# VectorE's eviction of the own-rows product moved behind the copy of the next turned tile, in a graph network with three layers on one core

## The reference

```python
deg = jnp.maximum(segment_sum(ones, dst), 1.0)
h = layernorm(x)
for l in range(3):
    h_neigh = segment_sum(h[src], dst) / deg
    rst = relu(h @ W_self[l] + h_neigh @ W_neigh[l] + b[l])
    h = rst / max(norm(rst), 1e-12)
x = x + h
# then per row: layer norm, gate over 8 experts, the best two of them, layer norm
```

## Time and profile before

| | before |
|---|---|
| median of 3 runs | 2106.8 us (2105.93 to 2120.68) |
| profiled execution, time | 2109.54 us |
| profiled execution, span | 2107.5 us |
| granted TensorE clock, mean | 0.990 |
| TensorE matmul busy | 1983.7 us, 94% |
| VectorE busy | 1673.1 us, 79% |
| ScalarE busy | 1019.9 us, 48% |
| GpSimd busy | 1274.4 us, 60% |

### The profile page before, as it was taken

How to read it: one execution, slowest core, us unless ns; L and a number is a source line. 1 busy time by engine, 2 the same in 40 slices (tenths; PEclk the granted TensorE clock), 3 DMA queues, 4 the chain that set the end, 5 groups by cost and what they waited for, 6 DMA issues and landing times.

```text
span 2107.5 us, 43053 instructions
## 1 busy us (share of the span) xinstructions
PE 1983.7 (94%) x14767; PEld 1098.9 (52%) x14773; DVE 1673.1 (79%) x4118; ACT 1019.9 (48%) x1801; POOL 1274.4 (60%) x1396
## 2 busy tenths in 40 slices
PE   6999899997999999999999999998899999999996
PEld 2444444443444444444444444444577777777774
DVE  7678986655777777776888878885699999999985
ACT  4444333333344344443444444554677776777751
POOL 2884116774566666664444444444578888888865
PEclk9999999998999999999999999999999999999999
DMA  6664348984887877864878887765778999899963
GB/s 205 171 169 132 123 139 135 145 126 113 194 195 195 189 202 194 193 191 148 244 245 250 245 250 234 223 219 184 216 165 176 176 186 170 178 179 180 172 100 49
DMA packets 307454, 379.27 MB, mean 180 GB/s; under 512 B 176825, under 2 KB 176999, under 8 KB 307239
## 3 DMA queue, kind: packets, MB, share of 16 engines
q1 hardware_dynamic: 246423, 211.09, 42.2%
q0 software_dynamic: 60816, 165.43, 32.1%
HBM read 175.81 MB, written 165.31 MB: 162 GB/s over the span
## 4 chain that ended last, share of the span: by engine, by line
PE 45%; POOL 24%; issue 12%; DVE 8%; DMA 7%; ACT 4%; SPq 0%; POOLq 0%; DVEq 0%; ACTq 0%
PE psY L580 20%; PE psS L580 18%; DMA w_n<-HH 5%; POOL out_dram L924 4%; POOL node_info L759 4%; POOL X L852 3%; PE psT L1799 2%; POOL zr L915 2%; POOL slot_table L759 2%; POOL G L836 2%; POOL area L836 2%; PE psY L1900 1%; POOL scl L905 1%; DVE R L1495 1%; PE psA L1859 1%
## 5 line engine op out<-in xcount | busy, mean ns | idle before, releaser
L580 PE MATMUL psY<-w_n,HT 128*128 128x512 f16 x1884 | 438.8, 383 | 31.6 <-DVE HT L1369 22.0
L580 PE MATMUL psS<-w_s,HT 128*128 128x512 f16 x1884 | 432.2, 379 | 0.0
L580 PEld LDWEIGHTS psY<-w_n,HT 128*128 128x128 f16 x1884 | 183.1, 99 | 265.2 <-DVE HT L1369 33.2
L1015 ACT ACTIVATE RR<-R 128x512 f32<-128x512 f32 x237 | 149.5, 631 | 311.3 <-DVE R L1495 311.2
L580 PEld LDWEIGHTS psS<-w_s,HT 128*128 128x128 f16 x1884 | 180.3, 98 | 199.4 <-issue 0.5
L868 POOL DMA_INDIRECT y_rows<-YB,poutT x158 | 161.8, 1024 | 197.8 <-DVE YB L1376 162.9
L1386 DVE SCALAR_TENSOR_TENSOR SB<-psS,downs,bias 128x512 f32<-128x512 f32 x237 | 177.7, 750 | 65.6 <-PE psS L580 64.8
L580 PE MATMUL psS<-w_w,raw 128*128 128x512 f16 x948 | 217.5, 379 | 0.8 <-ACT raw L1108 0.8
L861 POOL TENSOR_TENSOR scl<-ssm,halfpow 128x1 f32<-128x1 f32 x158 | 88.9, 562 | 195.0 <-DVE ssm L1513 195.0
L1376 DVE SCALAR_TENSOR_TENSOR YB<-psY,YB 128x512 f16<-128x512 f32 x237 | 162.6, 686 | 50.3 <-ACT YB L982 50.3
L1026 ACT ACTIVATE HH<-RR,scl 128x512 f16<-128x512 f32 x158 | 114.0, 722 | 150.4 <-POOL scl L861 150.4
(11 more groups left out here) (312 smaller groups left out, 4085.0 us busy)
## 6 DMA issues: line engine op xcount, KB each, us to landing
self_rows<-SB SPq DMA_DIRECT2D x236, 256.0 KB, 2.7
Sl<-self_rows SPq DMA_DIRECT2D x158, 256.0 KB
area<-in_x_dram SPq DMA_DIRECT2D x78, 256.0 KB, 4.1
y_rows<-YB SPq DMA_DIRECT2D x78, 256.0 KB
out_dram<-obb SPq DMA_DIRECT2D x78, 256.0 KB, 4.2
raw<-in_L_gnn_W_neigh_dram SPq DMA_DIRECT2D x12, 256.0 KB, 3.4
raw<-in_L_gnn_W_self_dram SPq DMA_DIRECT2D x12, 256.0 KB, 3.8
y_rows<-YB,poutT POOLq DMA_INDIRECT x158
```

The source lines that it names most:

```text
L580: mm = eng.matmul(acc, lhs[:, a, c, :], w[:, bpart, c, :], start=(c == 0 and n == 0), stop=(stop and c == KC - 1 and n == 2))
L1015: act.activation(RR[i][:, :], R[i][:, :], ACT.Relu).then_inc(s.rr, 1)
```

## The change

In the plans of VectorE for layers 1 and 2, `sev_early` is taken from the end of the list, where it had tile s, to the place behind `turn`, with tile s-1. In each step VectorE so evicts the own rows of the tile before, after it has made the one-hot matrix and copied the turned rows of tile s+1. The plan gets one step more at its end. Nothing else is changed.

```diff
-                run_plan(T, [(5, lambda t, l=l: one_hot(t, l)), (1, lambda t, l=l: turn(t, l)),
+                run_plan(T, [(5, lambda t, l=l: one_hot(t, l)), (1, lambda t, l=l: turn(t, l)), (-1, lambda t, l=l: sev_early(t, l)),
                                       (2, lambda t, l=l: hlo(t, l)), (0, lambda t, l=l: ylo(t, l)), (3, lambda t, l=l: carry_lo(t, l)),
                                       (3, lambda t, l=l: combine(t, l)), (3, lambda t, l=l: sum_squares(t, l)),
-                                      (3, lambda t, l=l: sum_floor(t, l)), (0, lambda t, l=l: sev_early(t, l))],
+                                      (3, lambda t, l=l: sum_floor(t, l))],
                          late_steps, run=l - 1)
```

## The result

| | before | changed |
|---|---|---|
| median of 11 runs | 2106.05 us (2102.48 to 2120.68) | 2125.65 us (2119.16 to 2131.31) |
| profiled execution, time | 2109.54 us | 2120.55 us |
| profiled execution, span | 2107.5 us | 2118.5 us |

The ratio of the two is 1.0081, with a 95% interval of 1.0067 to 1.0094: 0.8% slower, some 17 us. The profiled execution is one of the faster ones of the changed kernel; in it the loss is 11.0 us, so what follows places 11 of the 17 us.

What follows compares the result with a forecast made beforehand. TensorE was taken to bound the early parts, a loop without TensorE nearly to close the late ones. Terms -2.3 + 6 + 3 + 3 = +9.7 us on 2106.8 gave 2116.5, say 2117 us; range 2101 to 2131.

Steps and rivals of the forecast that it cites:

- Late parts: -2.3 forecast: Late parts: 1.0 us gained over 20 pairs, 1.3 us at the two layer ends; ends -13.2 and 0.
- A loop without TensorE: Late parts: a chain over power, hhi, late turn, yhi, ylo, carry, combine, only 0.05 us a pair shorter than TensorE's loop.
- rival (b): Late parts: the copy is the bound after all, gaining 13.2 us; about 2106 us; chance 0.08.
- Early layer 1: +6 and +3 forecast: Early layer 1: +6 us for DMA transposes issued later, +3 us for the store nearer ahead on their queue.
- the feedback: Early layer 1: a late transpose gives the next 7.02 us lead, afterwards 6.34; losing this costs +6 us, ends 0 and +9.2.
- Rival (a): Early parts: transposes behind a wait land under 6.34 us, in layer 2 under 5.7, so no loss; 2104.5 us; chance 0.17.
- The term that I had cut to a tenth: Early layer 1: the store 0.84 us nearer ahead of the transpose on SyncE's queue, +3 us, ends 0 and +28.6.
- Early layer 2: +3 forecast: Early layer 2: SyncE issues the transpose 0.61 us later, behind store, load and bias write; +3 us, ends 0 and 14.6.
- the fixed landing: Early layer 2: only the issue moves; no loss if transposes land 5.7 us after issue or sooner.
- Rival (c): Early layer 2: transposes have no slack, each pair takes 0.6 us more; 2128 us; chance 0.13.
- The upper end of 28.6 us: Early layer 1: all 34 odd tiles' transposes let the nearer store pass, at 0.84 us each.

Runs made afterwards that it cites:

- experiment 4: The kernel before with sev behind turn in the late parts alone, early parts as before: ratio 0.9985 (0.9968 to 1.0001).
- experiment 8: The kernel before with only ScalarE's yhi moved ahead of the late turn: ratio 1.0005 (0.9995 to 1.0015).
- experiment 1: The kernel before with sev behind turn in layer 1 alone, layer 2 as before: ratio 1.0043 (1.0026 to 1.0060).
- experiment 3: The changed kernel with SyncE's store of own rows behind the DMA transpose in both layers: ratio to the kernel before 0.9994 (0.9978 to 1.0009).
- experiment 9: The kernel before with the store of even tiles in layer 1 held back to stand near the transpose: ratio 1.0055 (1.0036 to 1.0074).
- experiment 2: The kernel before with sev behind turn in layer 2 alone, layer 1 as before: ratio 1.0037 (1.0021 to 1.0052).
- experiment 5: The kernel before with only SyncE's store of own rows moved behind the DMA transpose, both layers: ratio 1.0033 (1.0020 to 1.0045).
- experiment 7: The kernel before with sev behind turn in the late parts alone and ScalarE's yhi ahead of the late turn: ratio 0.9982 (0.9972 to 0.9992).
- experiment 10: The changed kernel with GpSimd's gather behind the scatter in layer 1's first 64 steps: ratio to the kernel before 0.9997 (0.9987 to 1.0006).

## Why the prediction came out as it did

The forecast was +9.7 us, 2117 us, 0.5% slower. The runs show 0.8%, some 17 us, 2125.65 us in the median; the one profile shows +11.0. The direction held, and the rows foretold which instruction would stand where. That the terms add up to nearly what the profile shows is in part luck: layer 1 was put 2.3 us too high and layer 2 3.3 us too low, and neither size came from the mechanism as I had given it.

**Late parts: -2.3 forecast, -2.1 measured.** A loop without TensorE closes them; pairs fell by 0.06 us, not 0.66. The critical view shows the change from one loop to the other, experiments 4 and 8 agree, and rival (b) is out. The wait for the copy fell to 0.65 us only, where I expected about 0.4.

**Early layer 1: +6 and +3 forecast, +6.7 measured (+8.0 in experiment 1).** The sum is near, but its two parts are the wrong way round. The step that failed is the feedback, "today a late transpose makes the next one early in relation to TensorE", whose loss I put at +6 us: the lead did fall from 7.02 to 6.36 us as worked out, but experiment 3 has that lead and no loss. Rival (a) was right on this point, that a transpose behind a wait lands in under 6.34 us: in the changed kernel it took 3.8 to 5.2 us, and waits still come in every second pair only, when I expected nearly every one. What I had left out is that the wait delays the transpose and not GpSimd's gather, so that the later transpose has the gather out of its way. The term that I had cut to a tenth, the store nearer by 0.84 us, carries the layer's loss (experiments 3 and 9).

**Early layer 2: +3 forecast, +6.3 measured (+7.4 in experiment 2).** As foretold, SyncE issues the transpose behind three others, 0.6 to 0.7 us later than before. But the working let only the time of issue move and held the landing as it was: "nothing if they land 5.7 us after issue or sooner". In the order of before they land after 4.6 us, so by that sentence there would have been no loss. The step that failed is the fixed landing: it grew by 1.0 us, to a median of 5.6 and up to 6.7, and 9 `neigh` of 24 waited. The later issue was needed for that too: with the old lead of 6.34 us most of these landings would have been in time. Rival (c), no slack at all, would have had nearly all of them wait; rival (a), under 5.7 us, held before the change and not after it.

**Why both went wrong** is one reading. I took the earlier trace rows, transposes in time behind three transfers, as a sign that what goes ahead on the queue costs little, and a landing as a property of the transpose. It depends on what runs beside it: in layer 2, 3.6 us with nothing just ahead (experiment 5), 4.6 behind three transfers (experiment 7, same order on VectorE). The rule of the Trainium skill ("DMA: Bandwidth & Descriptors", queues, rings and completion order), that descriptors of one issuing queue are consumed in ring order on each engine, fits this 1.0 us, though transfers that merely share the engines would cost time as well, and no run tells the two apart. The upper end of 28.6 us, which I had drawn from the rule by charging every transpose 0.84 us, did not come: the price in layer 1 was 7 to 10 us, and in the changed kernel only every second transpose came late.

## What to carry to other kernels

When a stage is moved on one engine, look at the queues of the engines that wait for it, and at what runs beside their transfers: here a 0.75 us eviction moved by 0.87 us changed what stood around a DMA transpose, and the transpose took 1.0 us longer to land besides going out 0.7 us later. The slack of a transfer that nobody waited for holds for its old surroundings only: 4.6 us of landing in 6.34 us of lead were not enough for a lead of 5.66 us. A shorter wait of an engine on a copy is a gain only if no other loop is of nearly the same length: here 1.0 us of waiting hid a second loop that was 0.06 us shorter.

## What the runs showed of the hardware that I had not expected

A DMA transpose of 256 KB took 3.5 us from issue to landing with nothing just ahead of it on its queue (3.3 to 4.0, experiment 3; median 3.6 in experiment 5), 4.6 us with three transfers of 256 KB issued in the 1.5 us ahead of it (experiment 7), and 5.6 us (4.8 to 6.7) in the changed kernel, where the three were issued in the 1.4 us ahead and GpSimd's scatter followed 0.64 instead of 1.32 us behind. Why the last step costs another 1.0 us is open.

In layer 1 the landing swung between 3.8 and 8.4 us, and it went by how far ahead GpSimd's gather had been issued: 7.0 to 8.2 us where it was at most 0.06 us, 3.8 to 5.2 us where it was 0.8 us or more. So it alternated: with every lead at 6.36 us, a transpose issued after a pair with a wait, and so well behind its gather, never came late, and the one behind it nearly always did, 16 times in all, by 0.6 to 2.0 us. Moving the gather behind the scatter brought the landing to a median of 3.7 us (experiment 10), and the one transpose there that had the gather just ahead of it again came 2.42 us late. What in the gather holds up the transpose no run shows.
